# Mixture-of-experts and attention block on one core: the first router's weights by way of PSUM, and one low part more on GpSimd

## The reference

```python
x = x + 0.5 * ffn(layernorm(x))     # 8 experts, top 2, d_model 512, d_ff 256
x = x + attention(layernorm(x))     # 16 heads of 32, 4 key/value heads, causal, RoPE
x = x + 0.5 * ffn(layernorm(x))     # the same weights again

def ffn(x):
    logits = x @ router_w.T
    topk_vals, topk_idx = top_k(logits, 2)
    w = softmax(topk_vals)
    out_e = (silu(x @ w1[e]) * (x @ w2[e])) @ w3[e]
    return sum over the two experts of w * out_e
```

## Time and profile before

| | |
|---|---|
| median of three runs | 1318.1 us (1316.18 to 1319.28) |
| the profiled execution, its own time | 1319.45 us |
| its span, first to last instruction | 1318.2 us |
| PE busy | 1183.2 us, 90% |
| DVE busy | 907.6 us, 69% |
| ACT busy | 660.7 us, 50% |
| POOL busy | 596.0 us, 45% |
| mean granted TensorE clock | 0.965 of full speed |

### The profile page before, as it was taken

The page is one execution under the profiler, slowest core; times in us unless marked ns, Lnnn a source line. Parts: engine busy times, 40 slices in busy tenths (PEclk is TensorE's granted clock), DMA queues, the critical chain, the costliest instruction groups (busy, mean ns, idle before and its releaser), DMA issues.

```text
span 1318.2 us, 21769 instructions
## 1 busy us (share of the span) xinstructions
PE 1183.2 (90%) x7252; PEld 770.6 (58%) x7252; DVE 907.6 (69%) x2104; ACT 660.7 (50%) x1313; POOL 596.0 (45%) x495
## 2 busy tenths in 40 slices
PE   4489999949998999999999999999999948999996
PEld 4468888828776554445545554445443437777774
DVE  8867777759997665575677776577663675666664
ACT  2535545526556554354455565356566832444442
POOL 4644445313210111001426556455673372888886
PEclk9689999979999999999999999999999978999998
DMA  9823333456540132023345834655733253666665
GB/s 341 329 81 108 109 112 106 128 162 107 94 68 4 33 67 34 1 79 67 82 129 130 161 97 97 192 125 144 150 97 65 87 181 107 101 102 104 101 103 74
DMA packets 66971, 146.92 MB, mean 111 GB/s; under 512 B 8784, under 2 KB 28240, under 8 KB 62864
## 3 DMA queue, kind: packets, MB, share of 16 engines
q0 software_dynamic: 35184, 93.34, 33.5%
q1 hardware_dynamic: 31680, 52.19, 11.5%
HBM read 79.71 MB, written 33.55 MB: 86 GB/s over the span
## 4 chain that ended last, share of the span: by engine, by line
PE 59%; DVE 18%; DMA 8%; issue 6%; POOL 5%; ACT 3%; SPq 0%; POOLq 0%; DVEq 0%; ACTq 0%
PE bank L827 10%; PE bank L1603 9%; PE bank L1615 9%; PE bank L984 8%; PE bank L850 5%; DMA out<-Y,DI 4%; PE bank L1631 4%; PE bank L1668 4%; DVE PM L997 3%; DMA XG<-xn,TK 2%; DVE bank L999 2%; POOL out L777 2%; PE bank L809 2%; POOL CH L1769 2%; PE bank L1376 2%
## 5 line engine op out<-in xcount | busy, mean ns | idle before, releaser
L1716 ACT ACTIVATE P<-bank 128x512 f32<-128x512 f32 (+3 forms) x640 | 304.4, 536 | 267.1 <-PE bank L1603 258.9
L997 DVE TENSOR_REDUCE PM<-bank 128x1 f32<-128x512 f32 x384 | 253.1, 685 | 87.9 <-PE bank L984 87.1
L984 PE MATMUL bank<-Ks,Qs 96*128 96x512 f32 (+3 forms) x640 | 238.3, 391 | 13.9 <-DVE PM L999 6.4
L1603 PE MATMUL bank<-Qs,Ks 98*128 98x512 f32 (+3 forms) x640 | 241.4, 407 | 2.9 <-ACT P L1716 1.5
L1603 PEld LDWEIGHTS bank<-Qs,Ks 98*128 98x128 f32 x640 | 117.1, 190 | 128.9 <-issue 65.1
L1755 POOL TENSOR_SCALAR_AFFINE_SELECT P<-P 128x512 f32<-128x512 f32 x64 | 42.6, 666 | 292.7 <-ACT P L1716 243.9
L999 DVE CUSTOM_DVE_ANT_0 bank<-bank,KB 128x128 f32<-128x128 f32 (+3 forms) x256 | 124.6, 498 | 54.8 <-PE bank L984 54.2
L984 PEld LDWEIGHTS bank<-Ks,Qs 96*128 96x128 f32 x640 | 120.7, 190 | 70.9 <-DVE PM L997 26.6
L1615 PE MATMUL bank<-P,V 128*32 128x512 f32 (+3 forms) x1280 | 151.5, 545 | 2.9 <-POOL P L1755 2.9
L1769 POOL TENSOR_TENSOR CH<-CH,P 128x512 f32<-128x512 f32 x108 | 138.1, 1394 | 16.8 <-ACT P L1716 16.2
L777 POOL DMA_INDIRECT out<-Y,DI x78 | 126.7, 1625 | 41.0 <-issue 31.6
(11 more groups left out here) (193 smaller groups left out, 1947.9 us busy)
## 6 DMA issues: line engine op xcount, KB each, us to landing
CD<-P POOLq DMA_DIRECT2D x17, 1024.0 KB, 7.1
xn<-XN SPq DMA_DIRECT2D x8, 1024.0 KB, 6.9
WR<-L_ffn_w POOLq DMA_DIRECT2D x16, 512.0 KB, 14.8
XO<-y POOLq DMA_DIRECT2D x8, 1024.0 KB, 9.5
WR<-L_ffn_w SPq DMA_DIRECT2D x16, 512.0 KB, 7.8
CD<-P SPq DMA_DIRECT2D x7, 1024.0 KB, 5.3
CD<-CH POOLq DMA_DIRECT2D x7, 1024.0 KB, 7.5
XA<-y POOLq DMA_DIRECT2D x24, 256.0 KB, 4.3
```

Source lines behind the costliest of these rows:

```text
L984: pe.matmul(bk(g, bank)[:, 0:n], g.Qs[b][0:96, G % 4 * 4 + h, c * P:c * P + P], g.Ks[0:96, G % 4, k * BQ:k * BQ + n], start=True, stop=Tru ...
L997: dve.tensor_reduce(dst, bk(g, bank)[:, 0:n], AX.X, ALU.max).then_inc(s(f"free{bank}"), 1)
L1603: pe.matmul(bk(g, bank)[:, o:BQ], g.Ks[0:98, G % 4, k * P:k * P + P], g.Qs[G // 4][0:98, G % 4 * 4 + j, o:BQ], start=True, stop=True).then ...
L1716: act.activation(a.P4[buffer_of(n)][:, j, o:BQ], bk(g, score_bank(g, i))[:, o:BQ], ACT.Exp, scale=scale).then_inc(s("exp"), 1)
```

## The change

The three steps from exp(b - a) to the two weights write into PSUM, and the factor 0.5 is folded in: 2 (1 + e), its reciprocal, and e times that. Two instructions go. The function serves both routers. `wd` becomes one row smaller. Before the first feed-forward, GpSimd makes five low parts (experts 0 to 4), VectorE that of expert 5 in between and those of 6 and 7 behind. TensorE's wait is set to (5, 3).

```diff
@@ -154,7 +154,7 @@
-    r.wd = small(f"wd{f}", [P, 3, NT])
+    r.wd = small(f"wd{f}", [P, 2, NT])
@@ -475,7 +475,7 @@
-    for e in range(4):
+    for e in range(5):
         pool_low(g, 0, e)
@@ -633,14 +633,11 @@
     dve.wait_ge(s(f"we{f}"), 1)
-    dve.tensor_scalar(r.wd[:, 2, :], r.wd[:, 1, :], 1.0, None, ALU.add).then_inc(rt.sem, 1)
+    dve.tensor_scalar(ps.we, r.wd[:, 1, :], 1.0, 2.0, ALU.add, ALU.mult).then_inc(rt.sem, 1)
     dve.wait_ge(rt.sem, rt.up())
-    dve.reciprocal(ps.we, r.wd[:, 2, :]).then_inc(rt.sem, 1)
+    dve.reciprocal(ps.WV[:, 0, :], ps.we).then_inc(rt.sem, 1)
     dve.wait_ge(rt.sem, rt.up())
-    dve.tensor_tensor(r.wd[:, 0, :], r.wd[:, 1, :], ps.we, ALU.mult).then_inc(rt.sem, 1)
-    dve.tensor_scalar(ps.WV[:, 0, :], ps.we, 0.5, None, ALU.mult)
-    dve.wait_ge(rt.sem, rt.up())
-    dve.tensor_scalar(ps.WV[:, 1, :], r.wd[:, 0, :], 0.5, None, ALU.mult).then_inc(rt.sem, 1)
+    dve.tensor_tensor(ps.WV[:, 1, :], r.wd[:, 1, :], ps.WV[:, 0, :], ALU.mult).then_inc(rt.sem, 1)
     dve.wait_ge(rt.sem, rt.up())
@@ -796,7 +793,7 @@
-    low = (4, 4) if f == 0 else (7, 1)
+    low = (5, 3) if f == 0 else (7, 1)
@@ -1979,10 +1976,10 @@
         def low0():
-            dve_low(g, 0, 4)
+            dve_low(g, 0, 5)
 
         g.routed[0] = dve_route(g, 0, g.R0, low0)
-        for e in range(5, NE):
+        for e in range(6, NE):
             dve_low(g, 0, e)
```

## The result

| | kernel before | with the change |
|---|---|---|
| median, measured together on one chip | 1317.86 us (1315.12 to 1319.53, 8 runs) | 1312.49 us (1310.22 to 1316.13, 8 runs) |
| ratio, 95% interval | | 0.9959 [0.9945, 0.9974] |
| the profiled execution, its span | 1319.45, 1318.2 | 1312.69, 1311.4 |
| mean granted TensorE clock | 0.965 | 0.969 |

The change is faster by 5.4 us, and the two profiled executions differ by 6.8. The same kernel measured a second time, against the kernel before measured anew beside it, gave a smaller gain. That belongs to the experiments.

A forecast was written before the change was run, and what follows sets the result against it. Bound: the chain through L636's 8 us wait on GpSimd. First low-part product from 74.91 to 69.27 gives 5.64 us, plus 0.18 in the second router: 1318.1 - 5.8 = 1312.3 us; own range 1311 to 1313.8, 8-in-10 range 1308.7 to 1314.6.

The forecast's parts named there:

- L636 at 0.19 us, the weights in three instructions: First router's weights: PSUM output removes the stall, two instructions go, L650 starts 8.05 us earlier, at 45.62.
- The second rival: L636: the SBUF source alone causes the wait, now to the end of five low parts; 3.6 us slower, 1321.7; chance 0.04.
- The fifth low part is free on GpSimd: GpSimd, first router: it runs from 52.88 to 57.38, long before the gather, and costs nothing on its own engine.
- VectorE's middle low part is held for what is left of GpSimd's: Between one-hot rows and tile list: wait bounded by 0 and 2.69 us, taken as 2.69, so it starts at 57.38.
- TensorE's cold start is next: First tile: VectorE no longer late; slow clock gives turns in 1.12 us, 1.88 to L827, low-part product 1.87 later.
- The clock's luck: First low-part product to second tile, 5.35 or 4.32 us: could give up to 1.03 or nothing; left out of the sum.
- The first tile's gain is the end's gain: After the first tile: TensorE is busy 187.24 of 196 us and tiles follow without waiting, so the end gains the same.
- So it should stand in all three: L636's stall, some 7.87 us of the gain, lies in a chain of the same instructions in every run.
- Moving the fifth low part gives back about 2.4 us: First router: the change of weights alone, GpSimd at four low parts, would gain 8.2 us; the fifth costs about 2.4.
- The first rival: VectorE's middle low part and GpSimd's fifth do not hinder each other: gain 8.5 us, 1309.6; chance 0.13.
- The third: Rival: part of the gain lost by a longer hold or a late gather; gain 3 to 5, near 1314; chance 0.05.
- The fourth: Rival: no change, as the first tile starts earlier but a later stage waits anyhow; chance 0.03.

The follow-up runs named there:

- again: The full change unchanged, measured and profiled a second time on another chip: 1315.4 us against 1317.84 for the kernel before, ratio 0.9982 [0.9961, 1.0003].
- The short case: Second profile of the unchanged kernel before: L636 took 3.08 us, let in where GpSimd's third low part ended; profiled execution 1318.48 us.
- the two long ones: First and third profiles of the unchanged kernel before: L636 took 8.06 us, let in behind GpSimd's fourth low part; 1319.45 and 1318.78 us.
- the weights alone: Kernel before with only the three weight instructions changed, GpSimd keeping four low parts: 1314.9 us, ratio 0.9979; measured again on another chip 1316.55, ratio 0.9992.
- 12 probes: Small VectorE additions ahead of L636 in two variants of the kernel before, GpSimd making all eight low parts in the first router: 1340.22 and 1339.0 us.
- the fifth low part alone: Kernel before with five low parts on GpSimd and three on VectorE, the five old weight instructions kept: 1315.86 us, ratio 0.9998 [0.9970, 1.0026].

## Why the prediction was right, and where it wasn't

The time came out at 1312.49 us, where 1312.3 was predicted. Step by step, counted from L589 on, to leave out the shift of the front (predicted times less 39.45, measured ones less 41.49):

| step | predicted | after | again (less 41.78) |
|---|---|---|---|
| VectorE's middle low part begins | 15.24 | 15.20 | 15.17 |
| it ends | 20.21 | 19.63 | 18.45 |
| first turns | 26.07 | 25.38 | 24.37 |
| first high-part product | 27.95 | 27.26 | 26.25 |
| first low-part product | 29.82 | 29.12 | 28.12 |

- **L636 at 0.19 us, the weights in three instructions.** Right: 0.17 us in every kernel with the output in PSUM. The cause is shown as well, by the one output moved alone. The second rival, a wait from the SBUF source, is out.
- **The fifth low part is free on GpSimd.** Right: it ends at 58.97 and the gather is issued at 63.41. It could be later than 57.38 because GpSimd's run had waited 1.57 us for a cast.
- **VectorE's middle low part is held for what is left of GpSimd's.** Right in kind: 4.43 and 3.28 us instead of 2.28, where about 4.97 was predicted. The size depends on where GpSimd's run lies against the router, and it came out smaller by 0.5 and 1.7 us. That is nearly the whole difference in the table.
- **TensorE's cold start is next.** Right in size: turns in 1.12 us, 1.88 to the first product, 1.86 to the low-part one, and no wait for VectorE. The reason given, about 7 us of idle time ahead of the turns, was not: it was 5.79 and 4.33 us. The short case of the kernel before had 4.30 us and turns in 1.11, the two long ones 4.38 and 4.34 and turns in 0.66. So the idle time alone does not decide, and what does is open. The clock's luck behind it, from the first low-part product to the second tile, was 5.05 and 4.42 us, inside the 4.32 to 5.35 allowed for.
- **The first tile's gain is the end's gain.** Right: from the first high-part product of the second tile to the projection's first product it is 199.2 to 200.5 us in every profile, before and after. Later stages vary by more: from there to the second router's weights 800.5 to 804.5 us, and the last stretch 208.9 to 212.8, in kernels that are the same there. That scatter hides effects of one to three microseconds in any one execution. From the second tile's first product to the end the three profiles of before take 1236.8 to 1238.7 us, the two of the full change 1235.7 and 1237.5, and the other kernels 1236.8 to 1240.9. So no loss behind the second tile shows for the full change, but one of a microsecond or two can't be excluded.
- **"So it should stand in all three".** Wrong, and this is the step that failed. The stall of the kernel before took 8.06, 3.08 and 8.06 us in three profiled executions. The sum was made against a long one. By the rows from L589 the change is worth 6.3 to 7.4 us against a long case and 1.9 to 2.9 against the short one. The 5.4 and 2.4 us measured can be mixtures of the two; how often each case comes is not shown. The 5.8 of the prediction came close to the first of them partly by luck: a gain of 2.4 us would have lain outside even the wide range, which began at 3.5.
- **"Moving the fifth low part gives back about 2.4 us".** Wrong. With it and without it the router takes the same (28.6 and 28.4 us on the mean). The step shifted the end of the list's products with the rest, to 58.44. They end at 61.00, 20.05 us behind L589 where 18.99 was assumed, since they run longer at 1.2 GHz. VectorE had no slack there: without the hold it waits 1.04 us for them, and a third late low part is then last by 0.21 us and more behind the tile list. Both eat what an unhindered middle low part would bring. The first rival's 1309.6 us falls with it: even with no hold at all, the weights alone had 1314.9 and 1316.55.
- **The other rivals.** The third, part of the gain lost on the way, did not come about by its own reasons: the middle low part was held for less than one GpSimd instruction, and from the gather's issue to the turns it took 3.46 us, where 3.55 was assumed. The fourth, no change, is out by the first measurement. In the second the interval ends at 1.0003.

## What to carry to other kernels

A small VectorE instruction with a long duration beside a busy GpSimd was a wait each time here. Look at its kind and at where its operands lie, and send its output to PSUM if it has one SBUF input and the next step is VectorE's own. Profile the kernel before more than once before a stall is put into a sum at its full size: a wait for another engine's instruction depends on how two timelines meet, and these move by microseconds between executions. When a stall goes, time again what ran with no slack beside it (here the list's products, at the low clock) rather than shift its old end.

## What the runs showed of the hardware that had not been expected

- **A missed turn.** VectorE was let in at the end of the very GpSimd instruction that it met in all 12 probes that met one, in the fifth low part alone, in one profile of before, in the one with a copy ahead of L636, and in every 128x512 scaling ahead of the second router (1.66 to 1.74 us, four in each profile). In two profiles of before it was let in one instruction of 4.50 us later. What they have in common is a GpSimd run that began without a wait, whose rows overlap by some 0.10 us instead of 0.02 to 0.08, and a question 0.98 us into its third instruction. None of these was shown to be the cause. A kernel that makes GpSimd's run begin without a wait every time was not tried.
- **A tiny instruction waits like a large one, if its form is the wrong one.** 16 numbers per partition wait to the end of GpSimd's instruction (3.26 us for a pair of SBUF inputs with a PSUM output, 3.18 for a TENSOR_SCALAR from SBUF to SBUF), as the 2048 of a low part do (4.43 us instead of 2.28). One SBUF input with the output in PSUM does not wait (0.17 us). Nor do, from SBUF to SBUF, a TENSOR_REDUCE of 64 numbers (L615, 0.22 us), a BATCH_NORM_STATS2 of 512 (L281, 0.69 us at 1052.75) and a TENSOR_SCALAR of one number (L294, 0.15 us). Where between one and 16 numbers the wait begins was not tried.
- **The clock answers to work that serves nothing.** With products of constants in TensorE's idle time the granted clock stood at 1.00 in the first router (50 to 68 us), where it had been 0.50 in part, and the two routers got 3.5 to 5.3 us shorter by their rows.
